# Output products of three attention layers split by halves of the heads instead of by tokens

## The chip, the cores and the metric

The kernel runs on one core of a Trainium2 chip, as one program. Its engines have queues of their own and run side by side: TensorE (PE) multiplies, with its weight loads listed apart as PEld; VectorE (DVE) and ScalarE (ACT) do elementwise work and read TensorE's results from PSUM; GpSimd (POOL) has little to do here; SyncE (SP) issues DMAs. An engine works through its own list in order and waits at semaphores for the others. The metric is device time in microseconds (us), lower is better.

## The reference, cut to what matters

128 boards of 64 squares with 256 features pass four layers: attention with 8 heads (layer 0), attention with 4 heads (layer 1), a graph layer (layer 2) and again attention with 4 heads (layer 3). Each layer normalises, takes the positive part and adds its result to x. What the change touches is the last line of each attention:

```python
h = jnp.maximum(_layernorm(x, axis=-1), 0.0)
q, k, v = split_heads(h @ Wq), split_heads(h @ Wk), split_heads(h @ Wv)
sim = jnp.where(mask, jnp.einsum('bhid,bhjd->bhij', q, k) * scale, neg)
attn = jax.nn.softmax(sim, axis=-1)
out = jnp.einsum('bhij,bhjd->bhid', attn, v)          # heads side by side: 256 values per square
x = x + out.transpose(0, 2, 1, 3).reshape(...) @ Wo + bo
```

## The kernel before

Four boards are a group: 256 squares ("tokens"), which are two tiles of 128 tokens (`TT` = 2). There are 32 groups; two are in flight at a time, in slot 0 and slot 1, and 16 turns of the main loop work through them. Names that end in 0 or 1 are buffers of that slot.

The work on a group is a fixed list of 145 steps (`STEPS`): the steps of layer 0, layer 1, layer 2 and layer 3. In the code the three attentions have the numbers a = 0, 1 and 2 (so a = 2 is layer 3). Each engine walks through the list for slot 0 and puts steps of slot 1, about half a list behind, in between, after numbers written out by hand in the table `ORDER`, one row of numbers per engine. Where two steps of one slot stand together on one engine, steps of the other slot may stand between them on another.

For float32 precision the operands of the large products are kept as a high and a low part, and each product is three matmuls: high times high weight, high times low weight, low times high weight.

At the end of an attention the steps are:

- `heads` 0 and 1: TensorE multiplies the probabilities of the first and of the second half of the heads with v, into PSUM. A half is 128 of the 256 values per token.
- `pv` 0 and 1: ScalarE copies a half as its high part to `oT` (line 924, semaphore `oT_hi`), VectorE takes the difference as its low part (line 989, `oT_lo`).
- `out` 0 and 1: TensorE multiplies `oT` with Wo (line 483, operands `w_hi,oT` and `w_lo,oT`). Before, step i makes the six products of the i-th tile of 128 tokens: both halves of the heads, high parts first, then the low parts. So the first step needs both halves, and the second waits for nothing. After each step's last matmul the semaphore `y_ps` goes up. PSUM bank 2 takes tile 0, bank 3 tile 1. They are the banks in which `heads` 0 left its result, and so the first step waits for the low part of half 0, too, which is the last reader there.
- `out` 0 and 1 on VectorE: it adds tile 0 and then tile 1 to x (line 1190), each after its own `y_ps`, then come the statistics of the next layer (lines 1091, 1097, 1099), the normalised xn (line 1103), and on TensorE the `turn` steps, which transpose xn (line 609). ScalarE and VectorE read these transposes as the high and low part of hT (lines 889 and 1117). In layer 2 the step `r` follows (`u_vec`), which waits for the parts of hT, and then `e`.
- `pt` (line 683) transposes the probabilities of a half of the heads; `ha` and `hat` belong to layer 2.

What stands between `out` 0 and `out` 1 on TensorE comes from the table: nothing in both slots' layer 0 and in slot 0's layer 1; the other slot's `pt` 0 of layer 3 in slot 1's layer 1; the other slot's two `turn` steps of layer 2 in layer 3 of both slots.

The function that the steps `out` and `g` share before:

```python
def tokens_out(o, actT, t, m, start=True, ready=(), halves=()):
    at = slice(t * P, t * P + P)
    for c in range(DC):
        if ready and t == 0:
            pe.wait_ge(ready[0], halves[c])
        mm(o, actT(0, c)[:, at], WHI[:, m, c, :], start and c == 0, False)
        mm(o, actT(0, c)[:, at], WLO[:, m, c, :], False, False)
    for c in range(DC):
        if ready and t == 0:
            pe.wait_ge(ready[1], halves[c])
        last = mm(o, actT(1, c)[:, at], WHI[:, m, c, :], False, c == DC - 1)
    return last
```

Of the kernel before, what the change touches and what calls it, by code (L numbers as in the profile page):

```python
# [29 lines left out]
P = 128  # L30
SQ = 64
D = 256
# [3 lines left out]
TT = TOK // P  # L36
# [70 lines left out]
H_BANKS, O_BANKS, Y_BANKS = (0, 3), (2, 0), (2, 3)  # L107
# [49 lines left out]
def build(nc, x_in, adjq_in, adjt_in, mats_in, cols_in, rows_in, cst_in, out):  # L157
# [8 lines left out]
    with ctx:  # L166
        def sb(name, shape, dt, scope=ctx):
            return scope.enter_context(nc.sbuf_tensor(name, shape, dt))
# [9 lines left out]
        WHI = sb("w_hi", [P, MATS, DC, D], F32R)  # L178
        WLO = sb("w_lo", [P, MATS, DC, D], F32R)
# [54 lines left out]
        Q, K, V, PR, PTS, OT, XP = ([] for _ in range(7))  # L234
# [35 lines left out]
        def bank(s, n):  # L270
            return PS[:, 4 * s + n, :]
# [42 lines left out]
        def units(a):  # L314


            first, blocks = ((0, 2), (4, 1), (6, 1))[a]
            return [(first + 2 * j + cj, 2 * j + cj, j, cj) for j in range(blocks) for cj in range(2)]

        def turned(a):  # L320

            us = units(a)
            return [us[0:2], us[2:4]] if len(us) == 4 else [us[0:1], us[1:2]]

        def norm_halves(a, v):

            return v.eight[2 * NORM_OF[a]:2 * NORM_OF[a] + 2]
# [56 lines left out]
        def alone(eng):  # L384


            eng.sem_inc(setup["waited"], 1)
# [93 lines left out]
        def _(pe):  # L481
            def mm(o, lhsT, rhs, start, stop):
                return nc.tensor.matmul(o, lhsT, rhs, start=start, stop=stop, skip_group_check=True)  # L483
# [121 lines left out]
            def transposed_h(s, a, t, v):  # L605

                pe.wait_ge(S[s]["xn_ready"], norm_halves(a, v)[t])
                for c in range(DC):
                    last = nc.tensor.transpose(bank(s, H_BANKS[c])[:, t * P:t * P + P],  # L609
                                               XN[s][:, t * D + c * P:t * D + c * P + P], IDENT)  # L610
                    if t == TT - 1:
                        last.then_inc(S[s]["hT_ps"], 1)

            def features_out(s, o, m, oc, halves=None):


                for c in range(DC):
                    if halves:
                        pe.wait_ge(S[s]["hT_hi"], halves[c])
                    mm(o, WHI[:, m, c, oc * P:oc * P + P], HT[s][:, 0, c, :], c == 0, False)  # L620
                    mm(o, WLO[:, m, c, oc * P:oc * P + P], HT[s][:, 0, c, :], False, False)
                for c in range(DC):
                    if halves:
                        pe.wait_ge(S[s]["hT_lo"], halves[c])
                    last = mm(o, WHI[:, m, c, oc * P:oc * P + P], HT[s][:, 1, c, :], False, c == DC - 1)
# [18 lines that stand above are left out]
            def att(s, k, a, i, v):  # L644
                sm, L, n = S[s], ATT[a], v.att[a]
                hd = D // L["heads"]
                two = L["heads"] == 8
                if k == "turn":
                    transposed_h(s, a, i, v)
                elif k in ("q", "k"):  # L650
                    b = 1 if k == "q" else 2
                    last = features_out(s, bank(s, b)[:, i * TOK:i * TOK + TOK], L["mats"] + b - 1, i,
                                        norm_halves(a, v) if k == "q" and i == 0 else None)
                    if i == DC - 1:
                        last.then_inc(sm[k + "_ps"], 1)
                elif k == "v":
                    last = tokens_out(bank(s, 3)[:, i * D:i * D + D], lambda j, c: HT[s][:, j, c, :], i, L["mats"] + 2)
                    if i == TT - 1:
                        last.then_inc(sm["v_ps"], 1)
                elif k == "scores":  # L660

                    pe.wait_ge(sm["q_sb"], n)
                    pe.wait_ge(sm["k_sb"], n)
                    alone(pe)
                    if two:

                        pe.wait_ge(sm["v_sb"], n)
                        alone(pe)
                    for b in range(NB):
                        for u, m, _, _ in units(a):  # L670
                            for half, h in enumerate(HEADS_AT[a][m]):
                                r, c = h * hd % P, h * hd // P
                                last = mm(bank(s, m)[SQ * half:SQ * half + SQ, b * SQ:b * SQ + SQ],
                                          Q[s][r:r + hd, c, b * SQ:b * SQ + SQ],
                                          K[s][r:r + hd, c, b * SQ:b * SQ + SQ], True, True)
                            if b == NB - 1:
                                last.then_inc(sm["s_ps"], 1)
                elif k == "pt":

                    for u, _, j, cj in turned(a)[i]:  # L680
                        pe.wait_ge(sm["probs"], v.eight[u])
                        for at in range(cj * TOK, cj * TOK + TOK, P):
                            last = nc.tensor.transpose(bank(s, 1 - i)[:, at:at + P], PR[s][:, j, at:at + P], IDENT)  # L683
                    last.then_inc(sm["pt_ps"], 1)
                elif k == "heads":

                    pe.wait_ge(sm["v_sb"], n)
                    pe.wait_ge(sm["pt_sb"], v.six[2 * a + i])
                    alone(pe)
                    place = {h: (m, half) for m, pair in enumerate(HEADS_AT[a]) for half, h in enumerate(pair)}  # L690
                    for t in range(TT):
                        for h in range(i * L["heads"] // 2, (i + 1) * L["heads"] // 2):
                            m, half = place[h]
                            _, _, j, cj = units(a)[m]
                            r, at = h * hd % P, cj * 256 + t * P + half * SQ
                            for e in range(2):
                                last = mm(bank(s, O_BANKS[i] + e)[r:r + hd, t * SQ:t * SQ + SQ],
                                          V[s][SQ * e:SQ * e + SQ, t, h * hd:h * hd + hd],
                                          PTS[s][SQ * e:SQ * e + SQ, j, at:at + SQ], True, True)
                    last.then_inc(sm["o_ps"], 1)  # L700
                elif k == "out":
                    if i == 0:

                        pe.wait_ge(sm["oT_lo"], v.six[2 * a])
                    tokens_out(bank(s, Y_BANKS[i])[:, 0:D], lambda j, c: OT[s][:, j, c, :], i, L["mats"] + 3,
                               ready=(sm["oT_hi"], sm["oT_lo"]), halves=v.six[2 * a:]).then_inc(sm["y_ps"], 1)

            def l2(s, k, i, v):
                sm, n = S[s], v.once
# [103 lines left out]
            def step(s, what, v):  # L813
                k, a, i = what
                if a == L2:
                    l2(s, k, i, v)
                else:
                    att(s, k, a, i, v)
# [481 lines left out]
```

## Time and profile before

| | us |
|---|---|
| three runs | 1987.11, 2001.88, 2002.51; median 2001.88 |
| the profiled execution | 1999.9 |
| its span (first to last instruction) | 1998.0 |
| TensorE busy in the span | 1842.2 (92%) |
| VectorE busy | 1381.1 (69%) |
| ScalarE busy | 996.2 (50%) |
| mean granted clock of TensorE | 0.966 |

A line of the timeline gives the start from the begin of the span and the duration in us, the engine, the line of the code, the instruction with what it writes and reads, and how many alike were merged (x2); the time of such a line goes from the first start to the last end. In square brackets is how long the engine was idle just before, and which instruction ended that. TensorE starts a matmul before the one ahead of it has ended, so their durations (about 0.28) are longer than the distance of their starts (about 0.12).

### The profile page before, as it was taken

The numbers are of one execution on the slowest core, as the hardware profiler recorded it, in microseconds if no ns is written. First come the engines' busy times: TensorE is split into PE (matmuls) and PEld (weight loads), VectorE is DVE, ScalarE is ACT, GpSimd is POOL, SyncE is SP. The second block draws the span as 40 slices with busy tenths as digits, with TensorE's granted clock in tenths as the row PEclk, the third lists the DMA queues.
The fourth block names the chain that finished last, engine by engine and source line by source line (L and its number), as shares of the span: only waits on it lengthen the run. The fifth ranks groups of instructions, "written<-read, shape, count | busy, mean of one in ns | idle before, by whom it ended". The sixth has DMA issues, their size and how long they took to land.

```text
span 1998.0 us, 58204 instructions
## 1 busy us (share of the span) xinstructions
PE 1842.2 (92%) x23623; PEld 1637.1 (82%) x23623; DVE 1381.1 (69%) x3777; ACT 996.2 (50%) x3707; POOL 153.1 (8%) x265
## 2 busy tenths in 40 slices
PE   7999999999999999999999999999999999999997
PEld 6787888887888887888888888888888888888886
DVE  4677677777677776667677667677677766767674
ACT  4545455445455545455445455445455545455452
POOL 0000000000000000000000000000000000000000
PEclk8999999999999999999999999999999989999898
DMA  6000000000000000000000000000000000000000
GB/s 196 1 13 8 13 13 8 12 13 8 13 13 8 12 13 8 13 13 8 12 13 8 13 13 8 12 13 8 13 13 8 11 13 8 13 13 8 12 7 6
DMA packets 36564, 30.62 MB, mean 15 GB/s; under 512 B 11600, under 2 KB 36176, under 8 KB 36368
## 3 DMA queue, kind: packets, MB, share of 16 engines
q1 hardware_dynamic: 36368, 27.48, 4.6%
q8 instruction: 187, 3.06, 0.6%
q14 instruction: 9, 0.07, 0.0%
HBM read 19.08 MB, written 8.39 MB: 14 GB/s over the span
## 4 chain that ended last, share of the span: by engine, by line
PE 75%; DVE 16%; ACT 4%; issue 4%; DMA 0%; DVEq 0%; SPq 0%; POOL 0%; POOLq 0%
PE ps L483 68%; PE ps L609 3%; PE ps L683 3%; DVE small L1091 2%; ACT probs L914 2%; DVE f L1250 1%; DVE f L1248 1%; DVE xn L1103 1%; DVE x L1255 1%; DVE oT L989 1%; DVE small L1097 1%; DVE kT L1150 1%; DVE probs L1164 1%; PE ps L806 1%; DVE probs L1180 1%
## 5 line engine op out<-in xcount | busy, mean ns | idle before, releaser
L483 PE MATMUL ps<-hT,w_hi 128*128 128x256 f32 x2560 | 487.7, 284 | 3.1 <-DVE hT L1117 1.4
L483 PE MATMUL ps<-w_hi,hT 128*128 128x256 f32 (+1 forms) x1536 | 423.8, 344 | 0.0
L483 PEld LDWEIGHTS ps<-hT,w_hi 128*128 128x128 f32 x2560 | 406.7, 190 | 6.7 <-DVE hT L1117 1.8
L914 ACT ACTIVATE probs<-probs,small 128x64 f32<-128x64 f32 x1024 | 342.1, 337 | 93.7 <-DVE small L1170 92.0
L483 PE MATMUL ps<-hT,w_lo 128*128 128x256 f32 x1280 | 332.8, 282 | 0.0
L483 PEld LDWEIGHTS ps<-w_hi,hT 128*128 128x128 f32 x1536 | 267.6, 188 | 42.6 <-DVE wh L1222 11.5
L470 POOL TENSOR_TENSOR small<-small,consts 128x1 f32<-128x1 f32 x256 | 151.1, 590 | 1818.6 <-DVE small L1099 1818.6
L483 PE MATMUL ps<-w_hi,oT 128*128 128x256 f32 x768 | 207.7, 335 | 56.4 <-DVE oT L989 47.5
L483 PE MATMUL ps<-w_lo,hT 128*128 128x256 f32 (+1 forms) x768 | 249.5, 337 | 0.0
L483 PEld LDWEIGHTS ps<-hT,w_lo 128*128 128x128 f32 x1280 | 243.7, 190 | 0.0
L483 PEld LDWEIGHTS ps<-w_hi,oT 128*128 128x128 f32 x768 | 150.0, 215 | 75.3 <-DVE oT L989 64.2
L914 ACT ACTIVATION_READ_ACCUMULATOR probs<-probs,small 128x1 f32 x1024 | 194.2, 190 | 0.0
L889 ACT ACTIVATE hT<-ps 128x256 fp32r<-128x256 f32 x256 | 86.1, 382 | 209.5 <-PE ps L609 209.5
L921 ACT ACTIVATE probsT<-ps 128x256 f32<-128x256 f32 (+1 forms) x192 | 87.7, 457 | 153.4 <-PE ps L683 149.9
L483 PEld LDWEIGHTS ps<-w_lo,hT 128*128 128x128 f32 x768 | 144.6, 188 | 10.7
L483 PE MATMUL ps<-probsT,v 64*64 64x64 f32 (+1 forms) x4096 | 95.7, 235 | 40.7 <-issue 40.7
L1190 DVE TENSOR_TENSOR x<-ps,x 128x256 f32<-128x256 f32 x192 | 81.3, 424 | 74.6 <-PE ps L483 74.3
L1117 DVE SCALAR_TENSOR_TENSOR hT<-ps,hT 128x256 fp32r<-128x256 f32 x256 | 98.0, 419 | 50.1 <-ACT hT L889 48.2
L483 PE MATMUL ps<-w_hi,ct_hi 128*128 128x256 f32 x512 | 127.0, 286 | 4.0 <-DVE ct_lo L1234 2.9
L483 PEld LDWEIGHTS ps<-probsT,v 64*64 64x64 f32 (+1 forms) x4096 | 68.4, 127 | 70.2 <-issue 60.4
L483 PE MATMUL ps<-w_lo,ct_hi 128*128 128x256 f32 x512 | 124.2, 281 | 0.9 <-issue 0.9
L609 PE MATMUL ps<-consts,xn 128*128 128x128 f32 x512 | 94.0, 299 | 31.9 <-DVE xn L1103 31.7
(128 smaller groups left out, 3330.5 us busy)
## 6 DMA issues: line engine op xcount, KB each, us to landing
x_next<-x SPq DMA_DIRECT2D x32, 256.0 KB, 2.6
out<-x SPq DMA_DIRECT2D x32, 256.0 KB, 2.2
raw_lo<-mats SPq DMA_DIRECT2D x6, 1024.0 KB, 10.0
adj<-adjq SPq DMA_DIRECT2D x64, 16.0 KB, 2.0
raw_hi<-mats SPq DMA_DIRECT2D x1, 1024.0 KB, 11.5
adjT<-adjt SPq DMA_DIRECT2D x64, 8.0 KB, 2.3
raw_lo<-mats SPq DMA_DIRECT2D x1, 512.0 KB, 8.2
raw_consts<-board_consts SPq DMA_DIRECT2D x1, 451.5 KB, 3.0
```

What stands on the lines that cost most here:

```text
L470: nc.gpsimd.tensor_tensor(RSTD[s][:, i:i + 1], VE[s][:, i:i + 1], HALF, ALU.pow).then_inc(sm["rstd"], 1)
L483: return nc.tensor.matmul(o, lhsT, rhs, start=start, stop=stop, skip_group_check=True)
L609: last = nc.tensor.transpose(bank(s, H_BANKS[c])[:, t * P:t * P + P], XN[s][:, t * D + c * P:t * D + c * P + P], IDENT)
L683: last = nc.tensor.transpose(bank(s, 1 - i)[:, at:at + P], PR[s][:, j, at:at + P], IDENT)
L806: last = nc.tensor.transpose(bank(s, HAT_BANKS[i])[:, t * P:t * P + P], F[s][:, t * D + i * P:t * D + i * P + P], IDENT)
L889: fn(HT[s][:, 0, c, :], bank(s, H_BANKS[c])[:, 0:TOK], ACT.Relu).then_inc(S[s]["hT_hi"], 1)
L914: last = fn(p, p, ACT.Exp, bias=ROWMAX[s][:, row:row + 1], accum_out=ROWSUM[s][:, row:row + 1])
L921: fn(PTS[s][:, j, at], bank(s, 1 - i)[:, at], ACT.Copy).then_inc(sm["pt_sb"], 1)
L989: return tt(o, full, hi.bitcast(F32), ALU.subtract)
L1091: nc.vector.bn_stats(STATS[s][:, t, :], (XP if a == 0 else X)[s][:, t * D:t * D + D]).then_inc(S[s]["bn"], 1)
L1117: stt(HT[s][:, 1, c, :], bank(s, H_BANKS[c])[:, 0:TOK], 0.0, HT[s][:, 0, c, :].bitcast(F32), ALU.max, ALU.subtract).then_inc(S[s]["hT_lo"], 1)
L1190: tt(X[s][:, at], bank(s, Y_BANKS[i])[:, 0:D], X[s][:, at], ALU.add).then_inc(sm["res"], 1)
```

## The change

The two steps of `out` no longer are the two tiles of tokens but the two halves of the heads. Step 0 multiplies the high and low part of half 0 for both tiles, step 1 those of half 1, adding to the sums in the same two banks. Each step waits for its own half alone. Since both tiles get their last matmul in step 1, `y_ps` goes up twice there, after the last two matmuls, and not at all in step 0. The number of matmuls, their shapes and operands are the same, and the table `ORDER` and all other engines' code are unchanged.

```diff
                 elif k == "out":
+                    def product(t, hi, w, start=False, stop=False):
+                        return mm(bank(s, Y_BANKS[t])[:, 0:D], OT[s][:, hi, i, t * P:t * P + P], w[:, L["mats"] + 3, i, :],
+                                  start, stop)
+
+                    pe.wait_ge(sm["oT_hi"], v.six[2 * a + i])
                     if i == 0:
                         pe.wait_ge(sm["oT_lo"], v.six[2 * a])
-                    tokens_out(bank(s, Y_BANKS[i])[:, 0:D], lambda j, c: OT[s][:, j, c, :], i, L["mats"] + 3,
-                               ready=(sm["oT_hi"], sm["oT_lo"]), halves=v.six[2 * a:]).then_inc(sm["y_ps"], 1)
+                    for t in range(TT):
+                        product(t, 0, WHI, start=i == 0)
+                        product(t, 0, WLO)
+                    pe.wait_ge(sm["oT_lo"], v.six[2 * a + i])
+                    for t in range(TT):
+                        last = product(t, 1, WHI, stop=i == 1)
+                        if i == 1:
+                            last.then_inc(sm["y_ps"], 1)
```

TensorE in layer 1 of slot 1 (`oT1`), with slot 0's transposes of probabilities of layer 3 (`probs0`) between the two steps; before, with the semaphores that an instruction waits for:

```order
L483 MATMUL ps<-w_hi,oT1 128x256 [waits oT_hi_1,oT_lo_1]
L483 MATMUL ps<-w_lo,oT1 128x256
L483 MATMUL ps<-w_hi,oT1 128x256 [waits oT_hi_1]
L483 MATMUL ps<-w_lo,oT1 128x256
L483 MATMUL ps<-w_hi,oT1 128x256 [waits oT_lo_1] x2
L683 MATMUL ps<-consts,probs0 128x128 [waits probs_0]
L683 MATMUL ps<-consts,probs0 128x128
L483 MATMUL ps<-w_hi,oT1 128x256
L483 MATMUL ps<-w_lo,oT1 128x256
```

The same place of TensorE in the changed kernel:

```order
L483 MATMUL ps<-w_hi,oT1 128x256 [waits oT_lo_1,oT_hi_1]
L483 MATMUL ps<-w_lo,oT1 128x256
L483 MATMUL ps<-w_hi,oT1 128x256
L483 MATMUL ps<-w_lo,oT1 128x256
L483 MATMUL ps<-w_hi,oT1 128x256 [waits oT_lo_1]
L483 MATMUL ps<-w_hi,oT1 128x256
L683 MATMUL ps<-consts,probs0 128x128 [waits probs_0]
L683 MATMUL ps<-consts,probs0 128x128
L483 MATMUL ps<-w_hi,oT1 128x256 [waits oT_hi_1]
L483 MATMUL ps<-w_lo,oT1 128x256
```

The waits for the second half have moved from ahead of slot 0's transposes to behind them.

VectorE in layer 3 of slot 1 (`oT1`, `x1`), with slot 0's normalised xn and hT of layer 2 between; these rows are the same before and after but for the line numbers, here those of before:

```order
L989 TENSOR_TENSOR oT1<-ps,oT1 128x256 [waits oT_hi_1]
L1103 TENSOR_SCALAR xn0<-x0,small0 128x256 [waits rstd_0]
L1190 TENSOR_TENSOR x1<-ps,x1 128x256 [waits y_ps_1,x_bias_1]
L1117 SCALAR_TENSOR_TENSOR hT0<-ps,hT0 128x256 [waits hT_hi_0] x2
L1190 TENSOR_TENSOR x1<-ps,x1 128x256 [waits y_ps_1,x_bias_1]
```

TensorE at the corresponding place of slot 0 in the changed kernel, from slot 1's `turn` (`xn1`) to the step `r` (`u_vec`):

```order
L609 MATMUL ps<-consts,xn1 128x128 [waits xn_ready_1]
L609 MATMUL ps<-consts,xn1 128x128
L483 MATMUL ps<-w_hi,oT0 128x256 [waits oT_hi_0]
L483 MATMUL ps<-w_lo,oT0 128x256
L483 MATMUL ps<-w_hi,oT0 128x256
L483 MATMUL ps<-w_lo,oT0 128x256
L483 MATMUL ps<-w_hi,oT0 128x256 [waits oT_lo_0]
L483 MATMUL ps<-w_hi,oT0 128x256
L483 MATMUL ps<-hT1,u_vec 100x256 [waits hT_hi_1] x2
L483 MATMUL ps<-hT1,u_vec 100x256 [waits hT_lo_1] x2
```

The instructions of VectorE have not moved, but its first add of the pair now waits for the last but one `oT0` row here, where before its semaphore went up ahead of the `turn`.

## Rows read from the trace of the kernel before

**Rows 1.** The page: busy us of each engine (share of the span) and instructions.

```profile
PE 1842.2 (92%) x23623; PEld 1637.1 (82%) x23623; DVE 1381.1 (69%) x3777; ACT 996.2 (50%) x3707; POOL 153.1 (8%) x265
```

**Rows 2.** The waits: who waited for whom, us in total, times, longest.

```profile
DVE x L1190 <- PE ps L483: 74.3, 138, 1.0
PE ps L483 <- DVE oT L989: 47.5, 71, 1.3
```

**Rows 3.** Timeline, layer 3 of slot 0: start, us, engine, line, instruction [idle before].

```profile
737.11 0.38 PE L483 MATMUL ps<-w_hi,oT 128*128 128x256 f32 x1 [0.93 <-DVE oT L989]
...
737.68 0.47 PE L483 MATMUL ps<-w_hi,oT 128*128 128x256 f32 x2
...
738.26 0.42 DVE L1190 TENSOR_TENSOR x<-ps,x 128x256 f32<-128x256 f32 x1 [0.24 <-PE ps L483]
...
738.90 0.40 PE L483 MATMUL ps<-w_hi,oT 128*128 128x256 f32 x2
738.93 0.76 DVE L1117 SCALAR_TENSOR_TENSOR hT<-ps,hT 128x256 fp32r<-128x256 f32 x2 [0.24 <-ACT hT L889]
...
739.14 0.97 PE L483 MATMUL ps<-hT,u_vec 128*100 128x256 f32 x4
...
739.95 0.28 PE L483 MATMUL ps<-hT,w_hi 128*128 128x256 f32 x1
```

**Rows 4.** Timeline of TensorE, then of VectorE, layer 1 of slot 1.

```profile
731.41 0.39 PE L483 MATMUL ps<-w_hi,oT 128*128 128x256 f32 x1 [0.38 <-DVE oT L989]
...
732.38 0.39 PE L483 MATMUL ps<-w_hi,oT 128*128 128x256 f32 x1 [0.46 <-ACT oT L924]
...
733.35 0.38 PE L683 MATMUL ps<-consts,probs 128*128 128x128 f32 x2
...
734.04 0.40 PE L483 MATMUL ps<-w_hi,oT 128*128 128x256 f32 x2
...
732.31 0.42 DVE L1180 TENSOR_TENSOR probs<-probs,small 128x256 f32<-128x256 f32 x1
...
733.63 0.42 DVE L1190 TENSOR_TENSOR x<-ps,x 128x256 f32<-128x256 f32 x1 [0.56 <-PE ps L483]
```

**Rows 5.** Timeline of VectorE, then of TensorE, layer 1 of slot 0.

```profile
674.41 0.42 DVE L1190 TENSOR_TENSOR x<-ps,x 128x256 f32<-128x256 f32 x1
...
672.65 0.39 PE L483 MATMUL ps<-w_hi,oT 128*128 128x256 f32 x1 [1.27 <-DVE oT L989]
...
673.91 0.50 PE L483 MATMUL ps<-w_hi,oT 128*128 128x256 f32 x2 [0.41 <-DVE oT L989]
```

**Rows 6.** Timeline of VectorE, then of TensorE, layer 0 of slot 0.

```profile
650.45 0.42 DVE L1190 TENSOR_TENSOR x<-ps,x 128x256 f32<-128x256 f32 x1 [0.29 <-PE ps L483]
...
653.35 0.41 DVE L1103 TENSOR_SCALAR xn<-x,small 128x256 f32<-128x256 f32 x1 [0.44 <-POOL small L470]
...
649.94 0.40 PE L483 MATMUL ps<-w_hi,oT 128*128 128x256 f32 x2
...
654.54 0.60 PE L609 MATMUL ps<-consts,xn 128*128 128x128 f32 x4
```

**Rows 7.** Windows: stretch, us, busy time of PE, PEld, DVE, ACT, POOL, granted clock.

```profile
78.19:1944.20 1866.01, 1740.85 (x22692) 1549.67 (x22693) 1318.14 (x3628) 946.63 (x3567) 146.32 (x248) 0.97 0.04 11
1400.25:1459.05 58.80, 54.96 (x734) 48.64 (x733) 42.33 (x118) 30.40 (x116) 4.79 (x8) 1.00 0.04 11
739.14:801.96 62.82, 58.34 (x734) 51.79 (x733) 43.13 (x119) 30.96 (x118) 4.60 (x8) 0.93 0.04 10
734.20:737.10 2.90, 1.46 (x36) 0.91 (x35) 2.52 (x10) 1.04 (x3) 0.89 (x2) 1.00 0.00 0
675.10:677.90 2.80, 1.42 (x37) 0.92 (x35) 2.42 (x10) 1.34 (x4) 0.91 (x2) 1.00 0.00 0
...
614.90:618.80 3.90, 2.45 (x44) 1.89 (x43) 3.49 (x13) 1.07 (x4) 1.20 (x2) 1.00 0.00 0
618.84:622.25 3.41, 3.41 (x18) 3.41 (x17) 2.03 (x5) 1.71 (x5) 0.00 (x0) 0.50 0.00 0
```

## The prediction

> **What bounds the kernel now.** I began with the page [rows 1]. TensorE is busy 92% of the span, VectorE 69%, ScalarE 50%. The two slots take turns on every engine, so TensorE nearly always has work; a change here can win only what TensorE waits, and loses whatever it makes TensorE wait anew. The waits come next [rows 2]: TensorE stands 47.5 us for the low parts of oT (VectorE's line 989), which is what the change is about; VectorE stands 74.3 us for finished output products before its residual add (line 1190), which the change also touches, since it decides when a product is finished. Whether either wait counts shows only at the single places, so I read the timeline around one `out` of each kind. Per turn of both slots there are six: each slot's layers 0, 1 and 3, sixteen turns in all. All readings are at the full clock.
>
> **Layer 3, the place that decides (31 of them: 16 in slot 0, 15 in slot 1 with the other slot's `turn` between its two `out` steps; the last one stands alone).** [rows 3] are slot 0's. TensorE starts the first `out` at 737.11, when the first low part is there, and nothing in it waits: the second half has come by the time it is wanted. So the change has no wait to remove here. But before, the first tokens' sum is complete at the end of this first step (last pair 737.68 + 0.47 = 738.15), and VectorE adds it at 738.26, while TensorE does slot 1's four transposes and the second `out`. VectorE then splits slot 1's hT at 738.93, two pieces, done at 738.93 + 0.76 = 739.69, and TensorE's `r` products, which begin at 739.14 and need those pieces, end in time for `e` at 739.95. In the order on VectorE the add of the first tokens stands ahead of both hT pieces. After the change that add waits for the second `out` too. Its last two matmuls begin at 738.90 and about 0.12 later; the first of them ends the first tokens' sum, at 738.90 + 0.28 = 739.18. The add follows a sum by 738.26 − 738.15 = 0.11, so it starts at 739.29. VectorE's instructions of this size take 0.42 each and start 0.34 apart back to back (the two hT pieces end 0.76 after the first start), so the hT pieces start at 739.63 and 739.97 and the last ends at 740.39 instead of 739.69. That is 0.70 us late, and `r`, whose four products would need only about 0.5 by themselves, already ended by this piece: `e` moves from 739.95 to 740.65. ScalarE's hTf (it needs hT's low part) and VectorE's second add with the statistics behind it move by about the same, so no engine is left that would give it back. So 31 × 0.70 = **21.7 us lost**; at the lower clock all products are longer, `r` too, and a tenth or two of it may lie under them.
>
> **Layer 1, slot 1 (16 places, [rows 4]).** Here TensorE does wait inside the first `out`: 0.46 for the second half's high part (732.38), and about 0.2 more for its low part. The change takes both waits off: the six products of the first half run from 731.41 to about 732.2. Behind them stand slot 0's two transposes of probs, which need the product that VectorE ends at 732.31 + 0.42 = 732.73; so TensorE waits there instead, until about 732.78. From the first transpose to the last pair of the second `out` it is 734.04 − 733.35 = 0.69, so the first tokens' sum ends at 732.78 + 0.69 + 0.28 = 733.75, and with a slow first transpose after the wait at 733.85. The add starts 0.11 later, at 733.86 to 733.96; before, it started at 733.63. From there VectorE runs through without a wait for another engine: scaling of probs, second add, statistics of both halves, and the oT piece for which TensorE's next `out` waits 0.93 until 737.11 [rows 3]. So although TensorE ends its second `out` 0.6 earlier, its next one starts 0.23 to 0.33 later. I take 0.30: 16 × 0.30 = **4.8 us lost**.
>
> **Layer 1, slot 0 (16 places, [rows 5]).** Both `out` steps stand together. The wait of 0.41 before 673.91 goes. But VectorE's first add starts at 674.41 without idle time, behind the scaling of the other slot's probs, and the new sum is complete at about 673.91 + 0.28 = 674.19 (the low part that ended the old wait, then one product; the ten products ahead of it, from 672.65 on, are through by then). VectorE therefore keeps its times, and with them the oT piece on which TensorE's next `out` hangs, at 677.90. TensorE ends 0.4 earlier and waits 0.4 longer: **0**.
>
> **Layer 0 (32 places, [rows 6]).** TensorE has the other slot's `ha` products ahead and waits for nothing. The first tokens' sum now ends with the last product but one, 649.94 + 0.28 = 650.22, so the first add starts at 650.33 and the second, 0.34 behind it, at 650.67 instead of 650.45: 0.2 late. What hides this: xn's second half, ready at 653.76, would be ready at 653.98, and TensorE asks for xn at 654.54, behind the other slot's products. Without that cover it would cost 32 × 0.2 = 6.4. **0**.
>
> No matmul, weight load or DMA is added or taken away: twelve products per `out` pair before and after, and one wait more, on a value long reached.
>
> **The clock.** The granted clock falls from 2.4 to 1.2 GHz (1.00 to 0.50) behind TensorE's emptiest stretch: it read 1.00 at 614.90 to 618.80 with 2.45 us busy of 3.90, and 0.50 right after [rows 7]. 31 half turns take 1866.01, 60.19 each, and one with the clock at 1.00 all through takes 58.80; so the falls cost about 31 × 1.39 = 43 us. The emptiest stretch, from the second `out` of layer 1 to the next slot's first `out`, becomes longer with the same work in it: 2.90 to 3.7 in one slot (ends 0.3 later, begins 0.5 earlier), 2.80 to 3.2 in the other. That is 20% on the mean, and I let the cost grow likewise: 43 × 0.2 = **9 us lost**, an estimate between 43 won (no fall any more) and 31 × (62.82 − 60.19) = 82 lost (every half turn like the one with 0.93 granted).
> The Trainium skill ("TensorE: Matmul & The Clock Gate", the table under "Why this matters for your kernels") warns of long idle gaps between bursts of matmuls as what drops the clock. Here the waits of the stretch are 0.93 and 1.27 us [rows 3, 5] and it falls all the same, so the trace shows less idle to be enough. By the page no new gap is long enough and this term would be 0, the sum 2026; by the rows it is 2035.
>
> **Sum.** The profiled execution took 1999.9 (span 1998.0), 2 under the median 2001.88. 1999.9 + 21.7 + 4.8 + 9 = 2035.4.
>
> **The rivals.**
> A, the forecast: 2035, chance 0.58. Its own range, with the layer 3 term between 0.5 and 0.75 and the clock between 0 and 20, is 2020 to 2048.
> B, the clock tips over: nearly every half turn pays the lower clock. Half of the bound of 82 gives 1999.9 + 26.5 + 41 = 2067. For it: the added waits all lie around the emptiest stretch. Against it: the new stop before `r` comes after 2 us of dense products. 0.12.
> C, not slower: the removed waits stay removed and the late add is hidden. It decides itself in layer 3: if the first tokens' sum were there 0.7 earlier, or the hT pieces did not queue behind the add. Then layer 1 gives back 16 × (0.46 + 0.2 + 0.41) = 17 and the time is 1983. For it: 47.5 us of waits exist. Against it: VectorE's order, and that VectorE, not TensorE, holds the chain from layer 1 to the next `out`. 0.07.
> The Trainium skill (the same page, its table of specifications) states that VectorE's queue is strictly first in, first out, which speaks against C; every timeline here agrees, VectorE's adds starting in program order.
> D, partly hidden: half of the 26.5 is swallowed, and the clock falls less often because its falls shift against the turns: 1999.9 + 13 − 2 = 2011. The runs of before, 1987.11 to 2002.51, show that such shifts are worth some us. 0.23.
> That the change does nothing holds only for layer 0 and is in the sum.
>
> **The numbers.** A and B and little of D are over 2022; D and a part of A lie within 1%, which is 1982 to 2022; C is on its edge. About 1% is also what a measurement can tell from no change. Faster 0.04, within 1% 0.24, slower 0.72. The range runs from D to near B, 2010 to 2060.
>
> **What would show it.** In the new profile: VectorE's wait at the add (now 74.3 us) grows by over 30, most of it in layer 3 where hT's start moves from 0.7 after the add's old start to directly behind the new one; TensorE waits about 0.6 to 0.7 in the `r` products, where it hardly waits now; TensorE's waits inside `out` for the second half vanish, and those before the transposes of probs and before layer 3's `out` grow; a half turn at full clock takes 59.7 instead of 58.8 to 59.2. Wrong would be: `e` starting no later after the `turn`, or a half turn at full clock not longer; then the sum falls. A mean granted clock of 0.966 or more would take away the 9 us.

## The result, and the profile after

The changed kernel takes 2022.39 us (median of four runs, 2018.65 to 2024.68), the kernel before beside it 1998.34 (1987.11 to 2002.51). The ratio is 1.0128, 95% interval 1.008 to 1.0175: slower by 1.3%, clear of the noise. The profiled execution took 2021.79, its span 2019.4, its mean granted clock is 0.973.

The page after, which answers to [rows 1] (busy us, share of the span, instructions):

```profile
PE 1835.4 (91%) x23623; PEld 1628.0 (81%) x23623; DVE 1369.3 (68%) x3777; ACT 994.3 (49%) x3707; POOL 153.7 (8%) x265
```

No engine has more to do; the span is longer by 21.4 us. The waits after (who waited for whom, us in total, times, longest):

```profile
DVE x L1203 <- PE ps L483: 137.7, 81, 2.8
PE ps L483 <- DVE oT L1002: 56.7, 62, 1.4
ACT hTf L948 <- DVE hT L1130: 41.1, 32, 1.5
```

VectorE's wait at its add went from 74.3 [rows 2] to 137.7 us, and TensorE's wait for oT, which the change is about, from 47.5 to 56.7. ScalarE's hTf now waits 41.1 us for VectorE's hT, 32 times; before it was 7.0:

```profile
ACT hTf L935 <- DVE hT L1117: 7.0, 32, 0.2
```

The timeline of the changed kernel in layer 3, here of slot 1, at the full clock (start, us, engine, line, instruction, idle before); [rows 3] is the place in slot 0 before:

```profile
563.81 0.35 PE L483 MATMUL ps<-w_hi,oT 128*128 128x256 f32 x1 [0.76 <-DVE oT L1002]
...
564.36 0.39 PE L483 MATMUL ps<-w_hi,oT 128*128 128x256 f32 x2
...
564.59 0.60 PE L609 MATMUL ps<-consts,xn 128*128 128x128 f32 x4
...
565.50 0.40 PE L483 MATMUL ps<-w_hi,oT 128*128 128x256 f32 x2
...
565.74 0.45 PE L483 MATMUL ps<-hT,u_vec 128*100 128x256 f32 x2
565.90 0.42 DVE L1203 TENSOR_TENSOR x<-ps,x 128x256 f32<-128x256 f32 x1 [1.26 <-PE ps L483]
566.24 0.74 DVE L1130 SCALAR_TENSOR_TENSOR hT<-ps,hT 128x256 fp32r<-128x256 f32 x2
...
566.71 0.69 PE L483 MATMUL ps<-hT,u_vec 128*100 128x256 f32 x2 [0.52 <-DVE hT L1130]
...
567.24 0.28 PE L483 MATMUL ps<-hT,w_hi 128*128 128x256 f32 x1
```

VectorE idles 1.26 us before the add; the add starts 0.12 behind the end of tile 0's sum (565.50 + 0.28); hT follows 0.34 later; `r` stops in its middle for 0.52, and from its start to `e` it is 567.24 − 565.74 = 1.50 us, where [rows 3] give 739.95 − 739.14 = 0.81. Both slots agree: the median of the places at the full clock is 1.50 after and 0.80 to 0.81 before, in either slot.

Layer 1 of slot 1 after (TensorE, then VectorE, then TensorE); before it is [rows 4]:

```profile
617.55 0.36 PE L483 MATMUL ps<-w_hi,oT 128*128 128x256 f32 x1 [0.47 <-DVE oT L1002]
...
618.84 0.44 PE L683 MATMUL ps<-consts,probs 128*128 128x128 f32 x2 [0.35 <-DVE probs L1193]
...
619.59 0.40 PE L483 MATMUL ps<-w_hi,oT 128*128 128x256 f32 x2
...
619.99 0.42 DVE L1203 TENSOR_TENSOR x<-ps,x 128x256 f32<-128x256 f32 x1 [0.87 <-PE ps L483]
...
623.52 0.55 PE L483 MATMUL ps<-w_hi,oT 128*128 128x256 f32 x1 [1.09 <-DVE oT L1002]
```

The waits inside `out` are gone; one of 0.35 stands before the transposes of probs and one of 1.09 before the next `out`. From the first `out` to layer 3's it is 5.97 us; before it was 737.11 − 731.41 = 5.70.

Layer 1 of slot 0 after (TensorE, VectorE); before it is [rows 5]:

```profile
558.57 0.36 PE L483 MATMUL ps<-w_hi,oT 128*128 128x256 f32 x1 [1.36 <-DVE oT L1002]
...
560.24 0.42 DVE L1203 TENSOR_TENSOR x<-ps,x 128x256 f32<-128x256 f32 x1
```

The add follows the first `out` by 1.67, before by 1.76; the next `out` follows by 563.81 − 558.57 = 5.24, the same as 677.90 − 672.65 = 5.25 before.

Windows of the changed kernel (stretch, us, busy time of PE, PEld, DVE, ACT, POOL, granted clock, then the share and the GB/s of DMA), one at a fall of the clock and one over 30 half turns (a half turn goes from one slot's `r` to the other's):

```profile
617.55:623.10 5.55, 3.45 (x48) 2.59 (x48) 4.09 (x15) 3.46 (x17) 0.56 (x2) 1.00 0.00 0
623.10:626.51 3.41, 2.99 (x14) 3.02 (x15) 1.25 (x4) 0.66 (x2) 0.63 (x1) 0.50 0.03 5
626.51:684.54 58.03, 53.21 (x720) 47.02 (x719) 41.23 (x115) 29.87 (x113) 4.41 (x8) 1.00 0.04 11
...
138.69:1964.79 1826.10, 1679.20 (x21963) 1491.86 (x21961) 1262.59 (x3510) 912.44 (x3451) 142.16 (x240) 0.98 0.04 11
```

A fall, a stretch in which the granted clock is 0.50, begins 0.42 us before layer 3's first `out` (623.52), inside TensorE's wait of 1.09, and lasts 3.41 us.

To tell the clock from the waits I use two figures for each kernel, both from its trace over the same 30 half turns: the sum that they would take at the full clock (stage by stage, the median of the places where 1.00 was granted throughout), and what is left of the total, which I call the cost of the falls. Where the stages are cut moves this split by about 2 us, and in a run below that has no fall in its 30 half turns 4 to 5 us are left all the same, so compare these costs and don't read one alone. Before: total 1803.1 = 1769 at full clock + 34. After: 1826.1 = 1792 + 34. So **the change cost 23 us of waits, and nothing of clock**, although the mean granted clock rose: over the 30 half turns 85 us were at 0.50, before 106.

### The profile page after: what moved, and what is told of

It reads as the page before. It is cut to its first block, busy times and chain, and to the rows that moved or that the text cites. A ratio compares the mean times of both kernels' runs of the same rounds, so it can differ in the third digit from the quotient of the medians.

```text
span 2019.4 us, 58204 instructions
## 1 busy us (share of the span) xinstructions
PE 1835.4 (91%) x23623; PEld 1628.0 (81%) x23623; DVE 1369.3 (68%) x3777; ACT 994.3 (49%) x3707; POOL 153.7 (8%) x265
## 4 chain that ended last, share of the span: by engine, by line
PE 73%; DVE 18%; issue 4%; ACT 4%; DMA 0%; DVEq 0%; SPq 0%; POOL 0%; POOLq 0%
PE ps L483 66%; PE ps L609 3%; DVE small L1104 3%; PE ps L683 3%; ACT probs L927 2%; DVE x L1203 2%; DVE small L1110 1%; DVE f L1263 1%; DVE xn L1116 1%; DVE f L1261 1%; DVE x L1268 1%; DVE kT L1163 1%; DVE oT L1002 1%; DVE small L1112 1%; DVE probs L1177 1%
## 5 line engine op out<-in xcount | busy, mean ns | idle before, releaser
L483 PE MATMUL ps<-w_hi,oT 128*128 128x256 f32 x768 | 195.3, 325 | 56.9 <-DVE oT L1002 56.7
L1203 DVE TENSOR_TENSOR x<-ps,x 128x256 f32<-128x256 f32 x192 | 77.7, 419 | 137.8 <-PE ps L483 137.7
L483 PE MATMUL ps<-probsT,v 64*64 64x64 f32 (+1 forms) x4096 | 91.1, 227 | 41.7 <-issue 40.4
```

The source lines that it names most:

```text
L1203: tt(X[s][:, at], bank(s, Y_BANKS[i])[:, 0:D], X[s][:, at], ALU.add).then_inc(sm["res"], 1)
```

## The experiments

Line numbers in rows of experiments differ by a few, the operands tell the instruction. All times are medians, each with the kernel before on the same chip.

### Layer 3 back to tokens, and layer 3 alone

The first kernel gives layer 3 its old steps, the second all layers but layer 3 (`a != 2`):

```diff
                 elif k == "out":
+                    if a == 2:
+                        if i == 0:
+                            pe.wait_ge(sm["oT_lo"], v.six[2 * a])
+                        tokens_out(bank(s, Y_BANKS[i])[:, 0:D], lambda j, c: OT[s][:, j, c, :], i, L["mats"] + 3,
+                                   ready=(sm["oT_hi"], sm["oT_lo"]), halves=v.six[2 * a:]).then_inc(sm["y_ps"], 1)
+                        return
```

> Layer 3 goes back to the split by tokens; layers 0 and 1 keep the split by halves. If the late residual add of layer 3 is the cause (theory 1), r to e takes 0.80 again at the full clock instead of 1.50 and only slot 1's layer 1 costs something, 16 x 0.27 = 4.3: about 2003 against 1998.3 of before. If the loss comes from layer 1, whose emptiest stretch before the next out is longer now (rival: 3.8 instead of 2.95 or 3.2), it stays near 2020. If it is the clock's falls over the dense products (rival), their cost would have to fall with the time.

Measured: 1991.29, before 1997.33, ratio 0.9974 (0.9952 to 0.9995). At full clock the 30 half turns take 1773, 4 more than before; the falls cost 18 instead of 34, which I had not expected.

> Layer 3 alone has the split by halves; layers 0 and 1 are as before. Theory 1: 31 x (0.70 - 0.09) = 19 us slower than before, about 2017, and r to e takes 1.50 at the full clock. Rival layer 1: near 2000. This run and the one with layers 0 and 1 alone should add up to the whole difference of 24 if the two places do not act on each other.

Measured: 2028.68, ratio 1.015 (1.0114 to 1.0187). At full clock 1788.5, that is 19 more than before; the falls cost 51 instead of 34. Its `r` stops as in the whole change:

```profile
1674.59 0.45 PE L483 MATMUL ps<-hT,u_vec 128*100 128x256 f32 x2
1675.56 0.69 PE L483 MATMUL ps<-hT,u_vec 128*100 128x256 f32 x2 [0.52 <-DVE hT L1136]
1676.10 0.28 PE L483 MATMUL ps<-hT,w_hi 128*128 128x256 f32 x1
```

The two halves of the change are told apart: nearly all of the loss by waiting is layer 3's. The measured times add up: 6.0 won and 31.4 lost make 25.3, and the whole change lost 24.1. And each half has an effect on the clock, of opposite sign, so that they cancel in the whole. In the profiled executions it is about 16 us each; by the medians of all runs it is nearer to 10, since the profiled execution of the first kernel (1987.52) was faster than its median and that of the second (2034.88) slower.

### The mechanism in layer 3: order on VectorE, and tile 0 earlier

If the loss is the queue on VectorE, putting both hT pieces ahead of the late add takes it away. The row of the table `ORDER` for VectorE (two places, one per slot):

```diff
-        6, 0, 2, 0, 5, 1, 1, 0, 0, 0, 1, 2, 1, 0, 4, 10, 0, 0, 0, 3, 0, 0, 0, 3, 0, 3, 0, 8, 0, 3, 0, 0, 0,
+        6, 0, 2, 0, 5, 1, 1, 0, 0, 0, 1, 2, 0, 0, 5, 10, 0, 0, 0, 3, 0, 0, 0, 3, 0, 3, 0, 8, 0, 3, 0, 0, 0,
...
-        1, 0, 0, 2, 0, 0, 5, 0, 1, 0, 1, 2, 0)),
+        1, 0, 0, 2, 0, 0, 5, 0, 1, 0, 3, 0, 0)),
```

> The whole change, with one thing turned round in VectorE's list: in layer 3 the other slot's two hT pieces now stand ahead of the first residual add. The sum of tile 0 is as late as in the change. Theory 1: the add no longer stops hT, r to e falls from 1.50 to 0.80 and 31 x 0.70 = 21.7 come back; but the adds, which before lay in idle time, now put the next statistics 0.34 later, of which TensorE's turn of layer 0 feels all in 16 places and part in the others, 5 to 8: about 2007 to 2009. If the late sum itself costs the time and not the queue behind it, or the clock, it stays near 2022.

Measured: 1998.80, ratio 1.0018 (1.0 to 1.0036). The timeline:

```profile
559.59 0.40 PE L483 MATMUL ps<-w_hi,oT 128*128 128x256 f32 x2
559.63 0.76 DVE L1130 SCALAR_TENSOR_TENSOR hT<-ps,hT 128x256 fp32r<-128x256 f32 x2 [0.90 <-ACT hT L902]
559.83 0.97 PE L483 MATMUL ps<-hT,u_vec 128*100 128x256 f32 x4
560.30 0.75 DVE L1203 TENSOR_TENSOR x<-ps,x 128x256 f32<-128x256 f32 x2
560.64 0.28 PE L483 MATMUL ps<-hT,w_hi 128*128 128x256 f32 x1
```

hT now waits for ScalarE alone, `r` to `e` is back at 0.81, and the two adds stand behind. Of the loss at full clock (23) 10 go, not 21: both adds now delay VectorE's later work, and from `e` to the next layer 1 `out` it takes 0.33 longer than in the changed kernel in every half turn. The other 14 of the 24 us won are falls (20 instead of 34).

The other remedy leaves VectorE alone and lets the second step finish tile 0 before it begins tile 1:

```diff
+                    if i == 1:
+                        product(0, 0, WHI)
+                        product(0, 0, WLO)
+                        pe.wait_ge(sm["oT_lo"], v.six[2 * a + i])
+                        product(0, 1, WHI, stop=True).then_inc(sm["y_ps"], 1)
+                        product(1, 0, WHI)
+                        product(1, 0, WLO)
+                        product(1, 1, WHI, stop=True).then_inc(sm["y_ps"], 1)
+                        return
```

> The whole change, with the six products of the second step in another order: all three of tile 0, then all three of tile 1, so that tile 0's sum is ready two products (0.24) earlier. Theory 1 is a matter of dose: r to e falls from 1.50 to about 1.26 in 31 places, and slot 1's layer 1 loses 0.03 instead of 0.27 in 16 places, together 7.4 + 3.8 = 11: about 2011. If the loss does not hang on when tile 0's sum is ready, nothing changes: 2022.

Measured: 1998.44, ratio 1.0005 (0.9987 to 1.0024). The timeline:

```profile
1521.07 0.43 DVE L1209 TENSOR_TENSOR x<-ps,x 128x256 f32<-128x256 f32 x1 [1.02 <-PE ps L483]
1521.15 0.45 PE L483 MATMUL ps<-hT,u_vec 128*100 128x256 f32 x2
1521.41 0.75 DVE L1136 SCALAR_TENSOR_TENSOR hT<-ps,hT 128x256 fp32r<-128x256 f32 x2
1521.88 0.69 PE L483 MATMUL ps<-hT,u_vec 128*100 128x256 f32 x2 [0.28 <-DVE hT L1136]
1522.41 0.28 PE L483 MATMUL ps<-hT,w_hi 128*128 128x256 f32 x1
```

The sum of tile 0 comes two products sooner, TensorE's stop shrinks from 0.52 to 0.28, and `r` to `e` is 1522.41 − 1521.15 = 1.26, as expected; the time of `e` follows that of the sum one for one. The rest of what was won is again falls: 23.

### Where the clock falls: layer 1's waits

To see whether TensorE's waits inside layer 1's `out` bring the clock down, the kernel before gets three products that nobody reads in slot 0's and slot 1's layer 1, so that TensorE works where it waited:

```diff
+            def fill(s, n, b=2, at=D):
+                for _ in range(n):
+                    mm(bank(s, b)[:, at:at + D], WHI[:, 3, 0, 0:P], WHI[:, 3, 0, :], True, True)
...
                     if i == 0:
                         pe.wait_ge(sm["oT_lo"], v.six[2 * a])
+                        if a == 1:
+                            fill(s, 3)
```

> The kernel before, with three more products in layer 1's first out, between the wait for the first half and the products proper; nobody reads their result, and they lie in the time in which TensorE waited 0.46 or 0.41 for the second half. Theory 2: the runs with layer 1 split lose 16 us less by the falls of the clock than before (18 to 23 of 30 half turns against 34), because TensorE no longer waits inside that out; then work put into the same waits does the same, the stage takes no longer at the full clock, and the time falls by 6 to 14: about 1987. If only the split order matters, or the falls have another cause, it stays at 1997, or 1 to 2 above.

Measured: 1983.77, before 1995.42, ratio 0.9927 (0.9898 to 0.9955). Work was added, and the kernel became 12 us faster. At full clock the half turns are about as long as before (1768); the falls cost 21 instead of 34. The trace records when the granted clock changes. Before, 12 of 25 falls begin 51.9 to 54.5 us behind the start of the last `r`, which is at layer 1's `out`, and 8 begin 57.5 to 58.1 behind it, at layer 3's `out`. Of the 12, five begin inside the waits that the change removes and seven in the matmuls just behind them. The longest falls are among these; the one in this row begins inside such a wait and fills nearly the whole stretch:

```profile
792.90:803.20 10.30, 9.20 (x65) 8.17 (x66) 6.66 (x23) 3.83 (x15) 1.10 (x2) 0.50 0.01 2
```

With the three products 3 falls begin at this place, and with layers 0 and 1 split by halves none does. That is where the gain by the clock comes from that layer 1's split brings. With layer 3 alone split, 22 of 30 falls begin here and 3 at layer 3's `out`: as long as layer 1 has its waits, the falls that layer 3's split adds come at layer 1.

### Where the clock falls: layer 3

The same in `r` of the changed kernel, four unread products in the new stop of 0.52:

```diff
+                        if j == 1:
+                            fill(s, 4, at=0)
                         for c in range(DC):
                             pe.wait_ge(ready, norm_halves(L2, v)[c])
```

> The whole change, with four more products that nobody reads in layer 2's r, in the wait of 0.70 for hT's low part. At the full clock r to e stays at 1.50. Theory 2: layer 3's late add costs twice, 21.7 us as waiting and some 16 by the clock's falls that this waiting adds; with the wait filled the second part goes: 2006 to 2014. If the falls do not hang on this wait: 2022 or, as the four products do not fit at the lower clock, up to 4 more.

Measured: 2024.54, ratio 1.015 (1.0116 to 1.0184): the stop is filled and nothing is won; the falls cost 34 as without the products.

```profile
564.25 0.45 PE L483 MATMUL ps<-hT,u_vec 128*100 128x256 f32 x2
...
564.54 0.65 PE L483 MATMUL ps<-w_hi 128*128 128x256 f32 x4
...
565.22 0.69 PE L483 MATMUL ps<-hT,u_vec 128*100 128x256 f32 x2
...
565.75 0.28 PE L483 MATMUL ps<-hT,w_hi 128*128 128x256 f32 x1
```

The products lie in the stop, and `r` to `e` stays at 565.75 − 564.25 = 1.50: the loss is the dependency, not TensorE's work. My theory that the new stop drops the clock fell. The trace says why: in the changed kernel 24 of 28 falls begin 57.1 to 58.9 us behind the last `r`, and the next `r` begins only at about 60. The falls begin ahead of the stop, at layer 3's `out`.

Two later runs fill the changed kernel's waits there and in layer 1, each by itself. Layer 3 alone:

```diff
+                    if a == 2 and i == 1 and v.once > 1:
+                        fill(1 - s, 4, 1)
                     pe.wait_ge(sm["v_sb"], n)
...
                 elif k == "out":
+                    if i == 0 and a == 2 and v.once > 1:
+                        fill(1 - s, ((8, 3), (7, 2))[a - 1][s], 3 - a)
```

> The whole change with unread products in layer 3's waits alone: 7 and 2 (slot 0 and slot 1) ahead of its output products and four ahead of its second heads, nothing in r and nothing in layer 1. In the trace of the changed kernel 24 of its 28 falls of the clock begin between 57.1 and 58.9 us behind the start of the last r, which is in the 2 to 3 us before the next r, at and ahead of layer 3's output products; where r itself was filled they began there too. Theory one, it is TensorE's waits at this place on which these falls hang: they go, 5 to 10 us of falls stay, 1994 to 2002. Theory two, the place is only where the clock's choice lands, and it takes in what lay up to 9 us before, layer 1's waits with it: part of the falls stay, 2005 to 2020.

Layer 1 alone (the second part of that edit, with `a == 1`):

> The other part: the whole change with unread products ahead of layer 1's output products alone, 8 and 3, nothing in layer 3 and nothing in r. Theory one (the falls hang on the waits in layer 3's last 3 us): they stay, 2015 to 2024. Theory two (what lay before counts as well): part of them go, 2000 to 2012.

Measured: 1996.88 (before 1998.27, ratio 0.9988, 0.9969 to 1.0007) and 2019.51 (1.0111, 1.0067 to 1.0156). The windows over 30 half turns, of layer 3 filled:

```profile
140.34:1939.93 1799.59, 1684.73 (x22211) 1495.53 (x22210) 1263.89 (x3510) 912.52 (x3451) 142.39 (x240) 1.00 0.04 11
```

and of layer 1 filled:

```profile
139.75:1961.91 1822.16, 1694.21 (x22127) 1504.97 (x22126) 1263.81 (x3510) 911.98 (x3451) 142.01 (x240) 0.98 0.04 11
```

Both have more matmuls (x22211, x22127) than the 21963 of the change, and where they stand decides: in layer 3 they bring the granted clock to 1.00 and the falls' cost to 7, in layer 1 the clock stays at 0.98 and the cost at 30. So theory one holds: in the changed kernel the falls hang on TensorE's waits ahead of layer 3's second heads and its output products, the last four us before `r`.

All of these places together, `r` among them:

> The whole change with unread products in TensorE's waits: ahead of layer 1's output products 8 and 3 of them (slot 0 and slot 1), ahead of layer 3's 7 and 2, four ahead of layer 3's second heads, four in r between the high and the low parts. It tells what the change costs with the clock's falls taken away. By my table a half turn of the changed kernel lasts 59.73 us at full clock (1792 for 30), and outside these 30 lie 196: with falls that cost 5 to 10, as in the best version (6.8, 1968), 1993 to 1999, that is 25 to 30 above that version, which is the 22.5 of the dependencies and the 1.1 by which the best one is shorter at full clock. If the 22.5 were no loss of dependencies but of clock too, it comes out within 10 of 1968. If filling doesn't reach the falls that come with layer 3's split (as filling r alone did not), 2010 or more.

Measured: 1993.23, before 1996.47, ratio 0.9988 (0.9976 to 1.0).

```profile
139.05:1935.38 1796.33, 1718.47 (x22496) 1525.64 (x22495) 1262.80 (x3510) 912.42 (x3451) 142.47 (x240) 1.00 0.04 11
```

No fall is left in the 30 half turns, and the total is 1796.33: the 1792 that I had put together from the stages at full clock, and 4 more, which no fall explains (some half turns take 60 to 61 us at a clock of 1.00). A half turn takes 59.75 in one slot and 59.73 in the other.

### Why layer 3's split brings more falls

The nine us ahead of `r` of slot 1 in the profile, with layer 3 split by tokens (the first kernel of the experiments):

```profile
550.16:559.16 9.00, 5.89 (x88) 4.96 (x81) 7.89 (x25) 5.76 (x25) 1.21 (x2) 1.00 0.01 2
```

and in the changed kernel:

```profile
556.74:565.74 9.00, 5.80 (x89) 4.89 (x81) 7.26 (x23) 5.77 (x25) 1.20 (x2) 1.00 0.01 2
```

TensorE idles 9.00 − 5.89 = 3.11 us in the one and 9.00 − 5.80 = 3.20 in the other, nearly the same, yet 15 falls begin at layer 3's `out` in the one kernel and 24 in the other. What differs as well is the length of a half turn. To lengthen it without a wait, the kernel with layers 0 and 1 split gets six more products where TensorE is dense:

```diff
+                    if (k, a, i) == ("q", 0, 1):
+                        for _ in range(6):
+                            mm(bank(s, 1)[:, TOK:2 * TOK], WHI[:, L["mats"], 0, P:2 * P], HT[s][:, 0, 0, :], True, False)
```

> This is the kernel with layers 0 and 1 split by halves of the heads and layer 3 by tokens (1991 us), with six products more in every half turn, in the middle of layer 0's q, where TensorE has no wait; their sums are overwritten by the products that follow, so nothing reads them. They lengthen a half turn by about 0.70 us, as layer 3's split does, but leave TensorE no emptier anywhere. Six of 0.11 to 0.12 us in 32 half turns are 21 to 23 us. Theory one, the falls of the clock that come with layer 3's split hang on the length of the half turn (how the turns fall in step with the clock's choices): 22 more at full clock and some 16 more of falls, 2026 to 2032. Theory two, they hang on TensorE's waits behind layer 3's output products: 22 more and no falls more, 2011 to 2016. Below 2008 the products would lie beside something that I have not seen.

Measured: 2019.86, before 1996.47, ratio 1.0117 (1.0095 to 1.0139), which is between the two theories. The windows over 30 half turns, of this kernel and of the one without the six products:

```profile
136.02:1959.80 1823.78, 1688.61 (x22142) 1511.25 (x22142) 1268.86 (x3510) 912.42 (x3452) 142.47 (x240) 0.98 0.04 11
...
140.24:1931.86 1791.62, 1660.22 (x21962) 1481.11 (x21961) 1268.72 (x3512) 912.44 (x3452) 142.44 (x240) 0.99 0.04 11
```

The stretch is 1823.78 − 1791.62 = 32 us longer. At full clock the stage with the six products takes 0.66 longer in one slot and 0.74 in the other, 21 us in all, and no other stage differs by more than 0.03; so the falls cost 11 more. At layer 3's `out` 22 falls begin instead of 15, and 76 us are at the lower clock instead of 51 (85 in the changed kernel, whose falls cost 14 to 16 more). So length alone, with no wait added, brings most of the additional falls and some 70% of their cost. What brings the rest stays open, as does why the length counts.

### A version that beats both

Layers 0 and 1 by halves with tile 0 first, layer 3 by tokens as before:

```diff
                 elif k == "out":
+                    if a == 2:
+                        if i == 0:
+                            pe.wait_ge(sm["oT_lo"], v.six[2 * a])
...
+                    if i == 1:
+                        product(0, 0, WHI)
```

> Layers 0 and 1 split by halves, with tile 0's three products first in the second step; layer 3 by tokens as before. At the full clock layer 1 gains 0.05 and 0.09 in 16 places each (2.2 us) against before, where it lost 0.18 in slot 1 without the order by tiles, and the clock's falls cost some 16 less: 1984 to 1990, the best so far. If layer 1 has nothing to do with the falls: 1995.

Measured: 1986.26, ratio 0.9953 (0.9926 to 0.9979), 1769 at full clock and 22 of falls. The 2.2 us that I expected at full clock are not there: layer 1 gives the 0.06 and 0.09 in its two slots, but from layer 0's `out` to layer 1's it takes 0.10 longer in each.

The same with unread products in TensorE's waits of layers 1 and 3 (the edits shown for layer 3 alone, with `a > 0`):

> The kernel with layers 0 and 1 split and tile 0 first, with products that nobody reads put into TensorE's other waits of the emptiest stretch: 8 and 3 ahead of layer 1's out, 4 ahead of layer 3's second heads, 7 and 2 ahead of layer 3's out. Theory 2: the remaining falls (some 18 us) go in part, 1975 to 1982. If TensorE's waits there are not what drops the clock, it is as without them, 1987, or slower by what does not fit into the waits.

Measured: 1968.45, before 1995.42, ratio 0.986 (0.9833 to 0.9886).

```profile
137.62:1912.53 1774.91, 1703.37 (x22376) 1516.24 (x22375) 1267.03 (x3511) 912.52 (x3451) 142.37 (x240) 1.00 0.04 11
```

It has 413 matmuls more than the change in this stretch and TensorE is busy 24 us longer, and it takes 51.2 us less (1774.91 against 1826.10). One fall is left. Against this one, the changed kernel with its waits filled is 1993.23 − 1968.45 = 24.8 us longer, both with hardly a fall: the price of the change's dependencies, once more, and about 1 us by which the best version is shorter at full clock.

## Why the prediction was right, and where it was off

I forecast 2035 with a range of 2010 to 2060, slower by over 1%; it is 2022.39, ratio 1.0128. The case that came is A, the forecast, near the lower end of its own range (2020 to 2048); about 13 us of the sum are missing.

**Layer 3, 31 × 0.70.** Right in size and in mechanism. `r` to `e` grew from 0.81 to 1.50; the add starts 0.12 behind the sum (0.11 used) and hT 0.34 behind the add (0.34 used). The order on VectorE alone restores 0.81, and an earlier sum shortens it by as much as the sum is earlier. So the late sum with hT queued behind it is shown as the cause.

What I had wrong in the same place is that the first `out` of layer 3 holds no wait. [rows 3] show its last pair at 0.47, after the change it takes 0.39. The pair begins at 737.68, and the second half's low part is done only at 737.29 + 0.42 = 737.71, so it waited a little:

```profile
737.29 0.42 DVE L989 TENSOR_TENSOR oT<-ps,oT 128x256 fp32r<-128x256 f32 x1
```

This step now ends 0.09 sooner (medians: 0.79 from `out` to `turn` instead of 0.88), 31 × 0.09 = 2.8 us won that the sum doesn't have.

**Layer 1, slot 1, 16 × 0.30.** The next `out` starts 5.97 − 5.70 = 0.27 later: 4.3 us. The transposes wait 0.35, and the add comes 619.99 − 617.55 = 2.44 behind the first `out` instead of 2.22, as the working said.

**Layer 1, slot 0, and layer 0: 0.** Right for slot 0 (5.24 against 5.25). For layer 0 nearly so: at full clock it takes 0.08 and 0.09 longer from its `out` to layer 1's (23.62 against 23.54 in one slot, 23.99 against 23.90 in the other), and the stretch ahead of it is 0.07 and 0.03 shorter, which leaves about 1 us in all.

**The clock, 9 lost.** This is the step that failed; it came out at 0 (34 against 34), and that it came out so near to nothing is two effects that happen to cancel, not something that the working had seen. I let the falls grow with the emptiest stretch, from 43 us, which was too much already: the 58.80 of [rows 7] is one slot's half turn, the other's takes 59.07 at the full clock. The runs show two things instead. Before, about half of the falls began at layer 1's `out`, inside the waits that the change removes or just behind them; splitting layers 0 and 1 alone takes 10 to 16 us of falls off, a gain that I had not put into the sum although I had the removed waits in front of me. And layer 3's split adds about as much: in the whole change by falls that begin at layer 3's `out`, of whose cost the mere length of the half turn brings some 70%.
The Trainium skill ("TensorE: Matmul & The Clock Gate", the table under "Why this matters for your kernels") warns of long idle gaps between bursts; I had worked out 2026 by it. That is nearer to the 2022.39 than my 2035, but not because there is no fall: falls cost 34 us in both kernels, with no wait at these places above 1.4 us, and filling those waits takes nearly all of it away. So the trace and the runs differ from that table of the Trainium skill here.

**The sum, redone.** 21.7 + 4.3 − 2.8 = 23.2, and no clock: 1999.9 + 23.2 = 2023.1; the profiled execution took 2021.79.

**The rivals.** B (the clock tips over, 2067) didn't come; the half turns between falls stay at 1.00. C (not slower, 1983) didn't come, and its mechanism fell: where its condition is met, with the hT pieces ahead of the add, the whole change takes 1998.80. With layer 3 left as it was and tile 0 finished first the time is 1986.26, but it comes there by falls, not by the 17 us of waits that C wanted back: at full clock that kernel is within 1 us of before. D (2011) needed half of the lost 26.5 us hidden; 23 of them are there.

**The signs I had named.** VectorE's wait at the add grew by 63 (over 30 said). TensorE's stop in `r` is 0.52 (0.6 to 0.7 said). The half turn at full clock is 59.73 (59.7 said). The mean granted clock of 0.973 is above the 0.966 at which I said that the 9 us would go, and they went.

## What to carry to other kernels

Splitting a sum by its inputs instead of its outputs lets the products start sooner, but every output is then finished at the end: look at who reads the first output, and at what stands behind that reader on its in-order engine, before counting the wait that goes. When TensorE's clock falls, a table of time at the full clock and cost of the falls tells dependencies from clock; without it, two effects of 10 to 16 us that cancel are read as none. And a short wait of TensorE at the place where the falls begin can be worth filling with products that nobody reads; here the same products behind that place won nothing.

## What the runs showed of the hardware that I had not expected

- Added matmuls made the kernel faster: three unread products in layer 1's waits 1995.42 → 1983.77, and products in all of the waits lift the clock over 30 half turns from 0.98 to 1.00 (2022.39 → 1993.23 for the changed kernel).
- The clock falls at stretches with several waits of 0.4 to 1.4 us each, in the changed kernel mostly for 3.41 us, before for up to 10.2. The mean granted clock doesn't rank kernels: at 0.966 before takes 1999.9, at 0.973 the change takes 2021.79.
- Which places fall depends on the length of the half turn as well: 0.7 us more of dense work brought 22 falls instead of 15 at one and the same place.
